# A recurrent, mixture-of-experts and attention network: expert rows scattered to their token's place, x kept in token rows, wide one-hots, feed-forward on chunk pairs

## The chip, the cores and the metric

The kernel runs on one core of a Trainium2 chip. The metric is the device time of one execution in microseconds. In the profile PE is TensorE's matmul side, PEld its weight loads, DVE is VectorE, ACT is ScalarE, POOL is GpSimd and SP is SyncE, whose queue issues most DMAs.

## The reference

There are 8 sequences of 256 steps with width 512. Floats are kept in pairs of 16-bit parts (high and low) in the kernel, so most products are done twice or three times.

```python
# GRU over time; here the 16x128 state sequence is the (8, 256, 512) input x
h = gru_scan(cond, x)                     # L0_cond, 256 steps, 8 sequences
scores = h @ w_gate_router.T             # 8 experts
topk_scores, topk_idx = top_k(scores, 2); p = softmax(topk_scores)
y = sum over the 2 experts of p * (silu(h @ gate_e.T) * (h @ up_e.T)) @ down_e.T   # F = 192
x = x + y                                                                          # called x1 below
xn = rms_norm(x) * g * (1 + scale) + shift      # scale, shift from cond @ W_emb, per sequence
q, k, v = xn @ W_qkv; q, k = rms_norm(q), rms_norm(k)   # 16 heads of 32
o = softmax(q k^T / sqrt(32)) v;  o = o + o @ W_out
hidden = sigmoid(o @ Q(w1).T) * (o @ Q(w2).T)   # Q: weights to -1, 0, 1; 1408 wide
x = x + hidden @ Q(w3).T
```

## The kernel before

**Layout.** The hidden states `hx` are kept with the features on the partitions and (time, feature block, sequence) in the free dimension. There are `NG = 16` groups of 128 tokens, in time order: a group holds 16 steps of all 8 sequences.

**Stages.** The recurrence runs to about 870 us. Then the states are split into 16-bit parts, scored by the router and written as token rows to DRAM (`xrows`), while weights arrive in pieces through `load_piece` and are split (to about 922 us). `slots` works out, for each token and each of its two experts, its place in a list sorted by expert, in which each expert's part is filled up to whole tiles of 128; there are `TILES = 40` tiles. To turn places into a list of rows, VectorE makes 32 one-hots of the place within the tile (`hot_low`, L1025), GpSimd 32 one-hots of the tile times the token's number (`hot_tile`, L1130), and `rows_of_tiles` (L758) multiplies them into `rowu`.

**Expert loop** (952 to 1117 us). For each tile GpSimd issues an indirect gather of 128 rows of `xrows` (L1138), TensorE transposes them (`turn_x`), multiplies by gate and up weights (`gate_up`, L778), transposes the hidden values and multiplies by the down weights (`down`). ScalarE evacuates (`take_y`, L896) and SP writes the tile to `yrows` in sorted order.

**Mix stage** (to 1178 us). For each of 16 groups GpSimd gathers the two expert rows of each token (L1147, slot by slot), ScalarE scales the first by its probability (L902), VectorE adds the second scaled (`mix_parts`, L1070), TensorE transposes back to features (`turn_back`, L811), VectorE adds x, which SP loads transposed (`residual`, L1076), ScalarE squares (L908), TensorE sums over partitions with a matrix of ones (`sum_x`), ScalarE takes the root (L914) and VectorE a reciprocal of 128 columns (`invert_x`, L1081).

**Attention** (to 1655 us). One batch is one sequence. `norm_x(b)` multiplies the states by the reciprocal root (VectorE, L1554), applies scale and shift per feature block (ScalarE, L1449, four operations), copies to 16 bits (L1453) and subtracts for the low part (L1556). It stands ahead of the stage for b = 0, at the end of the stage's start for b = 1, and at the end of batch b - 2 for the others, ahead of the eviction of the output projection (L1525, L1650). `project` (L1301) reads the result.

**Feed-forward** (to the end). Blocks of 128 hidden rows (`HM = 11`) of the ternary weights are quantised: GpSimd makes the negatives (L1188, three per block), VectorE finishes them (L1196). The first two blocks are done during attention. Tokens go in 4 chunks of 512. For each chunk, TensorE does for each block 16 matmuls into banks `mt % 2` (L1758); ScalarE takes the sigmoid (L1791), VectorE the product (L1816), ScalarE the high part (L1798) and VectorE the low part (L1820). Then 4 x 22 matmuls (L1774) give the result with features on partitions, VectorE adds x1 (L1828) and SP writes it out. Every engine keeps the order in which its instructions are written; semaphores tie the engines.

## Time and profile before

| | us |
|---|---|
| median of 3 runs | 1911.33 (1908.6 to 1915.46) |
| profiled execution | 1910.28 |
| its span | 1908.5 |

```profile
PE 1644.0 (86%) x31563; PEld 1199.2 (63%) x31563; DVE 1189.3 (62%) x4147; ACT 921.8 (48%) x3237; POOL 574.9 (30%) x1811
```

The line gives each engine's busy time, its share of the span and its instructions. The share is a mean over stages with different limits.

### The profile page before, as it was taken

Reading aid. Unit: us, or ns where it says so; the run is one execution under the profiler, and the core shown is the slowest. Engines: PE = TensorE matmul, PEld = TensorE weight load, DVE = VectorE, ACT = ScalarE, POOL = GpSimd, SP = SyncE. Lnnn points to the kernel's source line nnn. Section 1 sums busy time; section 2 is a strip of 40 time slices with the busy share of each in tenths; the row PEclk is TensorE's granted clock in tenths of the full one; section 3 lists DMA queues with packets and bytes.
Section 4 is the critical chain, followed back from the end, with each engine's and each line's share of the span. In section 5 each row is a group of like instructions: output and inputs, shape, how many; then the busy total and the mean of one; then the engine's idle time right before and its main releaser. Section 6 shows DMA issues by size and latency. Waiting matters only on the chain. (4 is left out here: it accounts for less than half of the span.)

```text
span 1908.5 us, 76620 instructions
## 1 busy us (share of the span) xinstructions
PE 1644.0 (86%) x31563; PEld 1199.2 (63%) x31563; DVE 1189.3 (62%) x4147; ACT 921.8 (48%) x3237; POOL 574.9 (30%) x1811
## 2 busy tenths in 40 slices
PE   6999999999999989994399965687888887689998
PEld 2788888888888889984256643354545555434443
DVE  4677777767777777777445436566666666573223
ACT  4544454445544444446245434367766666422111
POOL 0233333323333333334522234133322333660000
PEclk9898889988899955555599978789988988799999
DMA  7001000110000000005444356000000000220000
GB/s 273 26 4 50 5 26 5 60 44 5 4 5 5 18 35 5 4 5 169 137 149 143 130 164 193 1 1 0 0 0 0 0 0 1 65 77 13 22 22 22
DMA packets 39057, 90.19 MB, mean 47 GB/s; under 512 B 5088, under 2 KB 13408, under 8 KB 38624
## 3 DMA queue, kind: packets, MB, share of 16 engines
q1 hardware_dynamic: 32992, 66.96, 10.1%
q0 software_dynamic: 5760, 18.88, 3.4%
q8 instruction: 226, 3.70, 0.8%
q14 instruction: 79, 0.65, 0.1%
HBM read 66.88 MB, written 18.87 MB: 45 GB/s over the span
## 5 line engine op out<-in xcount | busy, mean ns | idle before, releaser
L321 PE MATMUL bank<-arena 128*128 128x8 f16 x12288 | 503.7, 171 | 32.4 <-DVE arena L500 27.2
L324 PE MATMUL bank<-arena 128*128 128x16 f16 x12288 | 498.1, 183 | 3.0 <-issue 2.7
L321 PEld LDWEIGHTS bank<-arena 128*128 128x128 f16 x12288 | 422.4, 99 | 85.0 <-ACT bank L409 57.3
L324 PEld LDWEIGHTS bank<-arena 128*128 128x128 f16 x12288 | 415.9, 99 | 3.7 <-issue 3.3
L573 POOL TENSOR_TENSOR arena<-arena 128x16 f32<-128x16 f32 x512 | 116.8, 228 | 597.8 <-DVE arena L504 583.2
L379 ACT ACTIVATE arena<-arena 128x16 f32<-128x16 f32 x512 | 114.2, 223 | 353.8 <-DVE arena L483 353.8
L483 DVE TENSOR_REDUCE arena<-bank 128x16 f32<-128x48 f32 x512 | 99.4, 194 | 147.3 <-PE bank L324 147.3
L1758 PE MATMUL bank<-arena 128*128 (+1 forms) x704 | 154.4, 379 | 15.5 <-DVE arena L1816 13.6
L1301 PE MATMUL bank<-arena 128*128 128x512 f16 x576 | 146.0, 409 | 17.5 <-DVE arena L1556 13.3
L494 DVE TENSOR_TENSOR_SCAN arena<-arena,bank 128x64 f32<-128x64 f32 x512 | 146.9, 287 | 20.4 <-ACT arena L379 6.0
L500 DVE TENSOR_TENSOR_SCAN arena<-arena 128x48 f16<-128x48 f32 x512 | 134.1, 262 | 6.0 <-ACT arena L389 0.6
L294 PE MATMUL bank<-arena 128*128 128x512 f16 x432 | 133.6, 423 | 0.0
L1758 PEld LDWEIGHTS bank<-arena 128*128 128x128 f16 x704 | 68.0, 98 | 101.2 <-DVE arena L1196 12.6
L389 ACT ACTIVATE arena<-arena 128x16 f32<-128x16 f32 x512 | 119.2, 233 | 24.7 <-DVE arena L494 4.7
L385 ACT ACTIVATE arena<-arena 128x16 f32<-128x16 f32 x512 | 110.3, 215 | 35.1 <-DVE arena L488 3.1
L488 DVE TENSOR_REDUCE arena<-bank 128x16 f32<-128x48 f32 x512 | 105.9, 207 | 26.3 <-PE bank L324 1.9
L1695 POOL TENSOR_TENSOR arena<-arena 128x512 f16<-128x512 f32 x64 | 79.3, 1247 | 130.6 <-ACT arena L1494 130.6
L504 DVE TENSOR_TENSOR_SCAN arena<-arena 128x48 f32<-128x48 f32 x512 | 117.1, 229 | 0.4
L1301 PEld LDWEIGHTS bank<-arena 128*128 128x128 f16 x576 | 59.5, 104 | 89.7 <-issue 24.5
L1791 ACT ACTIVATE arena<-bank 128x512 f32<-128x512 f32 x44 | 26.3, 597 | 176.1 <-PE bank L1758 176.1
L574 POOL COPY arena<-arena 128x16 f32<-128x16 f32 x512 | 110.9, 217 | 0.0
L509 DVE TENSOR_TENSOR arena<-arena 128x16 f16<-128x16 f32 x512 | 95.7, 187 | 17.7
(186 smaller groups left out, 2756.9 us busy)
## 6 DMA issues: line engine op xcount, KB each, us to landing
yrows<-arena SPq DMA_DIRECT2D x40, 256.0 KB
arena<-in_wgu SPq DMA_DIRECT2D x8, 768.0 KB, 5.9
arena<-in_xT SPq DMA_DIRECT2D x4, 1024.0 KB, 5.3
xrows<-arena SPq DMA_DIRECT2D x16, 256.0 KB, 4.8
arena<-in_xT SPq DMA_DIRECT2D x16, 256.0 KB
out_y<-arena SPq DMA_DIRECT2D x16, 256.0 KB, 2.0
arena<-in_wih SPq DMA_DIRECT2D x4, 768.0 KB, 8.6
arena<-in_whh SPq DMA_DIRECT2D x4, 768.0 KB, 5.2
```

The lines of the kernel that those rows point to most:

```text
L294: mm = nc.tensor.matmul(bank[7][:, :], wihs[:, wp, k, mt, :], xs[:, xp, k, :], start=(i % 12 == 0), stop=(i % 12 == 11))
L321: mm = nc.tensor.matmul(dst[:, j * B:(j + 1) * B, 1], w, h[:, 0], start=home not in opened, stop=False, skip_group_check=True)
L324: mm = nc.tensor.matmul(dst[:, j * B:(j + 1) * B, 1:3], w, h.rearrange("p a c -> p c a"), start=home not in opened, stop=False, skip_group ...
L379: A.activation(fn[:, HALF[g], 3], rzp[:, 0, HALF[g]], ACT.Sigmoid, scale=1 / SWX).then_inc(r_act[g], 1)
L389: A.activation(inh[:, HALF[g], 0], sn[:, HALF[g], 3], ACT.Tanh, scale=1 / SWX).then_inc(n_act[g], 1)
L494: V.tensor_tensor_scan(flat(sn[:, HALF[g]]), flat(fn[:, HALF[g]]), flat(gate_sums(t, 2, g)), 0.0, ALU.mult, ALU.add).then_inc(n_pre[g], 1)
L500: V.tensor_tensor_scan(flat(mv[:, t % 2, 0, HALF[g]]), flat(fh[:, HALF[g]]), flat(inh[:, HALF[g]]), 0.0, ALU.mult, ALU.add).then_inc(h_hi[ ...
L504: V.tensor_tensor_scan(flat(sh[:, HALF[g]]), flat(fh[:, HALF[g]]), flat(inh[:, HALF[g]]), 0.0, ALU.mult, ALU.add).then_inc(h_f32[g], 1)
L573: G.tensor_tensor(inh[:, HALF[g], 1], zeros[:, :], sh[:, HALF[g], 2], ALU.subtract)
L574: G.tensor_copy(inh[:, HALF[g], 2], sh[:, HALF[g], 2])
L1301: mm = nc.tensor.matmul(bank[5 + i % 2][:, :], xn[:, x_, k, half * P:(half + 1) * P], wqs[:, w_, k, col:col + D], start=(n == 0), stop=(n ...
L1758: mm = nc.tensor.matmul(bank[2 * a + mt % 2][:, :], w12[:, mt, a, k, :], o2p[:, part, k, bass.ts(c, CH)], start=(n == 0), stop=(n == 2 * K ...
```

## The change

**Scatter.** The list of rows now carries more: for each place the row of its token, whether it is the token's first or second expert (`pair`), and its probability in two parts. From these `goals` works out the row of `yrows` to which each place goes, `2 * token + (0 or 1)` in an order that puts tokens sequence by sequence; places that no token fills go to spare rows. `take_y` scales by the probability, and GpSimd scatters the tile with an indirect DMA. The two rows of one token thus lie side by side, and SP loads them for 128 tokens with one plain DMA.

**List of rows.** VectorE makes all one-hots in wide operations; GpSimd makes only two wide products for the probabilities (`hot_rest`), ahead of its gathers. `rest_of_tiles` stands on TensorE behind the first `gate_up`.

**Token rows.** x is loaded into SBUF as token rows (`xres`, over the states) during the expert loop. The two expert rows are added on GpSimd, the residual is added in token rows, and the sum of squares is along the free dimension (ScalarE, with an accumulated output). After the root and the reciprocal, ScalarE scales the rows, TensorE transposes them, and VectorE applies scale and shift on the way out of PSUM into `xnf`, for all sequences at once. `norm_x` is then only the split into two parts.

**Feed-forward.** Chunks go in pairs: for each block of weights the matmuls of two chunks. The down product takes the hidden values as weights and gives token rows. Loops over chunks are written out.

The core of the diff (constants, semaphores, memory layout and host arithmetic left out; `hdp` grows to two chunks):

```diff
-                for i in range(TILES):
-                    sp.wait_ge(y_evac, i + 1)
-                    sp.dma_start(yrows[i * P:(i + 1) * P, :], yo[:, i % 3, :]).then_inc(y_out[i % 3], 16)
+                sp.wait_ge(hc_lo, NG)
+                for g in range(NG):
+                    sp.dma_start(xres[:, g, :], xtok[g * P:(g + 1) * P, :]).then_inc(xres_in, 16)
...
+                    sp.dma_start(yb[:, g % 4], yrows[2 * g * P:2 * (g + 1) * P, :].rearrange("(p a) d -> p a d", a=2))\
+                        .then_inc(yb_in[g % 4], 16)
...
+                def rest_of_tiles():
+                    pe.wait_ge(slot_step, SLOT_STEPS["pair hot"])
+                    pe.wait_ge(part_hot, 2)
+                    for i in range(2 * NG):
+                        a, g = divmod(i, NG)
+                        mm = nc.tensor.matmul(bank[7][:, 0:3 * TILES], hot_low[:, a, g, :],
+                                              hot_rest[:, a, g].rearrange("p c t -> p (c t)"),
...
-                    A.activation(yo[:, i % 3, :], bank[6 + i % 2][:, :], ACT.Copy, scale=1 / SWX).then_inc(y_evac, 1)
+                    A.activation(yo[:, i % 3, :], bank[6 + i % 2][:, :], ACT.Copy, scale=share[:, i:i + 1]).then_inc(y_evac, 1)
+                def sum_squares(g):
+                    A.activation(square[:, :], xres[:, g, :], ACT.Square, accum_out=ssq[:, g:g + 1]).then_inc(sq_done, 1)
+                def root(g):
+                    A.activation(rms[:, g:g + 1], ssq[:, g:g + 1], ACT.Sqrt, scale=1 / D,
+                def unit_rows(g):
+                    A.activation(unit_x[:, g % 2, :], xres[:, g, :], ACT.Copy, scale=rinv[:, g:g + 1])\
...
-                    for i in range(2 * NG):
-                        a, g = divmod(i, NG)
-                        V.tensor_scalar(hot_low[:, a, g, :], iota, lowf[:, a, g:g + 1], None,
+                    V.tensor_tensor(hot_tile.rearrange("p a g t -> p (a g) t"),
...
+                    V.tensor_tensor(hot_row[:, :, :, :], hot_tile[:, :, :, :],
...
+                    for i in range(4):
+                        a, g = divmod(8 * i, NG)
+                        V.tensor_tensor(hot_low[:, a, g:g + 8, :], iota.unsqueeze(1).broadcast_to((P, 8, P)),
...
+                def residual(g):
+                    dve.wait_ge(ysum_done, g + 1)
+                    V.tensor_tensor(xres[:, g, :], xres[:, g, :], ysum[:, g % 2, :], ALU.add).then_inc(x1_done, 1)
+                def invert(g):
+                    V.reciprocal(rinv[:, g:g + 1], rms[:, g:g + 1]).then_inc(rinv_done, 1)
+                def adaptive(g):
+                    for k in range(KT):
+                        op = V.tensor_scalar(xnf[:, b, k, half * P:(half + 1) * P], bank[4 + g % 2][:, k * P:(k + 1) * P],
+                                             ada[:, 0, k, b:b + 1], ada[:, 1, k, b:b + 1], ALU.mult, ALU.add)
...
-                    G.tensor_scalar(hot_tile[:, a, g, :], iota[:, 0:TILES], tilef[:, a, g:g + 1], token[:, g:g + 1],
+                pool.wait_ge(slot_step, SLOT_STEPS["shares"])
+                for part in range(2):
+                    G.tensor_tensor(hot_rest[:, :, :, 1 + part, :], hot_tile[:, :, :, :],
+                                    prs[:, part].unsqueeze(3).broadcast_to((P, 2, NG, TILES)), ALU.mult)\
...
+                def scatter(i):
+                    pool.wait_ge(y_evac, i + 1)
+                    G.indirect_dma_start(out=yrows, out_offset=bass.IndirectOffsetOnAxis(ap=goal[:, i:i + 1], axis=0),
+                                         in_=yo[:, i % 3, :], in_offset=None).then_inc(y_out[i % 3], 16)
+                def sum_rows(g):
+                    pool.wait_ge(yb_in[g % 4], 16 * (g // 4 + 1))
+                    if g >= 2:
+                        pool.wait_ge(x1_done, g - 1)
+                    G.tensor_tensor(ysum[:, g % 2, :], yb[:, g % 4, 0, :], yb[:, g % 4, 1, :], ALU.add)\
+                for i in range(TILES + 6):
+                    if i < TILES:
+                        gather(i)
+                    if i >= 6:
+                        scatter(i - 6)
...
                 def norm_x(b):
-                    act.wait_ge(xnt_done, b + 1)
-                    for k in range(KT):
-                        A.activation(xnf[:, k, :], xnf[:, k, :], ACT.Identity, scale=ada[:, 0, k, bass.ds(b, 1)],
-                                     bias=ada[:, 1, k, bass.ds(b, 1)]).then_inc(xnf_done, 1)
-                    A.activation(xn[:, 0], xnf[:, :, :], ACT.Copy).then_inc(xn_hi, 1)
+                    A.activation(xn[:, 0].rearrange("p k s -> p (k s)"), xnf_of(b), ACT.Copy).then_inc(xn_hi, 1)
...
-                    V.tensor_tensor(xnf[:, :, :], x1, r, ALU.mult).then_inc(xnt_done, 1)
...
+                def up(pair, mt, cc):
+                    u, c = 2 * (pair * HM + mt) + cc, 2 * pair + cc
+                    if pair == 0 and cc == 0:
+                        pe.wait_ge(q_done, 3 * mt + 3)
+                    if u >= 2:
+                        pe.wait_ge(hdf_done, u - 1)
...
+                def down(pair, cc):
+                    for j in range(KT):
+                        v = (2 * pair + cc) * KT + j
+                        if v >= 2:
+                            pe.wait_ge(y_done, v - 1)
...
+                                mm = nc.tensor.matmul(bank[4 + j % 2][:, :], hdp[:, cc, part, mt, j * P:(j + 1) * P],
+                                                      w3q[:, mt, :], start=(n == 0), stop=(n == 2 * HM - 1))
...
+                for pair in range(2):
+                    for mt in range(HM):
+                        for cc in range(2):
+                            up(pair, mt, cc)
+                    for cc in range(2):
+                        down(pair, cc)
```

## Rows read from the trace of the kernel before

**Rows 1.** View by stretches: us, engines' busy us (instructions), granted TensorE clock, DMA share, GB/s
```profile
952.00:1117.00 165.00, 162.17 (x1192) 97.78 (x1191) 73.22 (x170) 78.59 (x166) 34.95 (x37) 0.99 0.41 134
1117.00:1178.00 61.00, 32.93 (x192) 25.93 (x192) 35.72 (x51) 25.76 (x49) 30.66 (x33) 0.83 0.73 211
```

**Rows 2.** Feed-forward stage: groups by line, whole run; then timeline and chain (start, us)
```profile
L1758 PE MATMUL bank<-arena 128*128 (+1 forms) x704 | 154.4, 379 | 15.5 <-DVE arena L1816 13.6 <-PEq L1266 1.8
L1774 PE MATMUL bank<-arena 128*128 128x512 f16 x352 | 77.3, 379 | 5.0 <-DVE arena L1828 5.0
...
1655.44 3.61 PE L1758 MATMUL bank<-arena 128*128 128x512 f16 x16 [1.83 <-PEq L1266]
...
1709.06 1.02 DVE arena L1828
1728.66 0.70 DVE arena L1816
1729.41 34.71 PE bank L1758 x160
1904.83 1.01 DVE arena L1828
```

**Rows 3.** Groups by line of 1655 to 1705 us: busy us, mean ns | idle before
```profile
L1188 POOL TENSOR_SCALAR arena<-arena,thr 128x512 f16<-128x512 f32 x27 | 43.4, 1625 | 12.8 <-POOLq L1266 12.4 <-DMA arena<-in_w3T 0.4
L1196 DVE SCALAR_TENSOR_TENSOR arena<-arena,thr 128x512 f16<-128x512 f32 x27 | 27.2, 1029 | 6.9 <-POOL arena L1188 6.9
L1820 DVE TENSOR_TENSOR arena<-arena 128x512 f16<-128x512 f32 x9 | 8.4, 938 | 0.0
```

**Rows 4.** Timeline where the list of rows is made: start us, us, engine, line
```profile
928.22 17.71 POOL L1130 TENSOR_SCALAR arena<-cst,arena 128x40 f16<-128x40 f32 x32 [12.22 <-DVE arena L1018]
928.37 6.37 DVE L1025 TENSOR_SCALAR arena<-cst,arena 128x128 f16<-128x128 f32 x32
...
946.79 1.17 POOL L1138 DMA_INDIRECT arena<-xrows,arena  x1 [0.87 <-DVE arena L1035]
```

**Rows 5.** Prices by width: VectorE groups by line, and GpSimd's L1126 (ns min/median/max)
```profile
L1010 DVE TENSOR_TENSOR arena<-arena 128x128 f32<-128x128 f32 x2 | 0.5, 288 | 0.0
L1028 DVE TENSOR_TENSOR arena<-cst,arena 128x320 f32<-128x320 f32 x1 | 0.5, 474 | 0.0
...
L1126 POOL TENSOR_TENSOR arena<-arena x16: 1147/1186/2204, 871.2 to 914.1; 128x512 f16<-128x512 f32 x16
```

**Rows 6.** View of the line that issues the gathers: ns min/median/max, time to landing
```profile
L1138 POOL DMA_INDIRECT arena<-xrows,arena x40: 941/944/1169, 946.8 to 1095.4; - x40
...
DMA to landing us min/median/max: 3.2/3.4/4.2
```

**Rows 7.** Timeline behind the experts: first gather, first use, and the last group's ring
```profile
1118.66 0.95 POOL L1147 DMA_INDIRECT arena<-yrows,arena  x1 [22.34 <-DMA yrows<-arena]
1123.46 0.72 ACT L902 ACTIVATE arena<-arena 128x512 f32<-128x512 f32 x1 [7.15 <-DMA arena<-yrows,arena]
...
1173.62 0.63 DVE L1076 TENSOR_TENSOR arena<-bank,arena 128x512 f32<-128x512 f32 x1
1174.28 0.63 ACT L908 ACTIVATE arena<-arena 128x512 f32<-128x512 f32 x1 [0.52 <-DVE arena L1076]
1176.16 0.37 ACT L914 ACTIVATE arena<-bank,epsb 128x128 f32<-128x128 f32 x1 [0.99 <-DVE arena L1081]
```

**Rows 8.** Timeline of the attention stage: first norm, second norm, end of a batch
```profile
1177.92 2.06 DVE L1554 TENSOR_TENSOR arena<-arena 128x1024 f32<-128x1024 f32 x1
1180.02 2.07 ACT L1449 ACTIVATE arena<-arena,ada 128x256 f32<-128x256 f32 x4 [3.49 <-DVE arena L1554]
1184.50 15.73 PE L1301 MATMUL bank<-arena 128*128 128x512 f16 x60 [8.38 <-DVE arena L1556]
...
1234.94 4.06 PE L1301 MATMUL bank<-arena 128*128 128x512 f16 x12 [4.96 <-DVE arena L1556]
...
1289.43 0.60 ACT L1525 ACTIVATE arena<-bank 128x512 f32 x1 [1.09 <-PE bank L1393]
```

More of the change, by code:

```diff
@@ L1785, in _, with gate, high @@
                 A = nc.scalar
[L1787 to L1802 removed]
+                def gate(u):
+                    act.wait_ge(up_mm, u + 1)
+                    A.activation(sgd[:, u % 2, :], bank[u % 2][:, :], ACT.Sigmoid, scale=1 / SX).then_inc(sgd_done, 1)
+                def high(u):
+                    pair, (mt, cc) = u // (2 * HM), divmod(u % (2 * HM), 2)
+                    act.wait_ge(hdf_done, u + 1)
+                    if pair == 1 and mt == 0:
+                        act.wait_ge(y_mm, (cc + 1) * KT)
+                    A.activation(hdp[:, cc, 0, mt, :], hdf[:, u % 2, :], ACT.Copy).then_inc(hdp_hi, 1)
+                for pair in range(2):
+                    for i in range(2 * HM):
+                        gate(2 * HM * pair + i)
+                        if i > 0:
+                            high(2 * HM * pair + i - 1)
+                    high(2 * HM * pair + 2 * HM - 1)
             @block.vector
@@ L1832, in _, with hidden @@
-                chunk(0, True)
-                with dve.Fori(1, NCH) as c:
-                    chunk(c, False)
-NAMES = ["xT", "condT", "wih", "whh", "bias", "wr", "wgu", "wdn", "wemb", "avec", "gqk", "wqkv", "wout",
+                def hidden(u):
+                    if u >= 2:
+                        dve.wait_ge(hdp_lo, u - 1)
+                    dve.wait_ge(sgd_done, u + 1)
+                    V.scalar_tensor_tensor(hdf[:, u % 2, :], bank[2 + u % 2][:, :], 1 / SX, sgd[:, u % 2, :], ALU.mult,
+                                           ALU.mult).then_inc(hdf_done, 1)
@@ new lines, in low, with result @@
+                def low(u):
+                    mt, cc = divmod(u % (2 * HM), 2)
+                    dve.wait_ge(hdp_hi, u + 1)
+                    V.tensor_tensor(hdp[:, cc, 1, mt, :], hdf[:, u % 2, :], hdp[:, cc, 0, mt, :],
+                                    ALU.subtract).then_inc(hdp_lo, 1)
+                def result(c, j):
+                    v = c * KT + j
+                    dve.wait_ge(y_mm, v + 1)
+                    if v >= 2:
+                        dve.wait_ge(y_out[j % 2], (c * 2 + j // 2) * 16)
+                    V.tensor_tensor(yo[:, j % 2, :], bank[4 + j % 2][:, :], xres[:, v, :], ALU.add).then_inc(y_done, 1)
@@ new lines, in _ @@
+                for pair in range(2):
+                    for i in range(2 * HM):
+                        mt, cc = divmod(i, 2)
+                        u = 2 * HM * pair + i
+                        if pair == 0 and mt + 2 < HM:
+                            quantise(dve, mt + 2, (0, 1) if cc == 0 else (2,))
+                        hidden(u)
+                        if i > 0:
+                            low(u - 1)
+                    low(2 * HM * pair + 2 * HM - 1)
+                    for c in (2 * pair, 2 * pair + 1):
+                        for j in range(KT):
+                            result(c, j)
```

368 lines of the change are left out of this document (173 added, 195 removed).

## Prediction

> **What bounds the kernel now.** I read the view by stretches first, cut where the stages end, then the chain that ended last, then the instruction timeline at the seams. The recurrence up to 870 us is not touched and neither is the splitting of weights and states up to 922 us. The expert loop is full of TensorE work: 162 of 165 us at a granted clock of 0.99 [rows 1]. The stage behind it is not: 61 us for sixteen row groups, with TensorE, VectorE and ScalarE each busy about half of it [rows 1]; work goes round in a ring there. In the last stage the chain is TensorE, broken by short waits [rows 2]. So each stage has a limit of its own, and each edit must be priced in its stage. The engines meet at the end of a stage, so a gain in one shifts all that follows.
>
> **Feed-forward on chunk pairs.** TensorE runs from 1655.44 us until the last add starts at 1904.83, some 249.3 us. It has 1056 matmuls of 512 columns in both kernels (704 up, 352 down); 160 in a row take 34.71 us, 0.217 each, so 229.2 us without waits. The idle time ahead of the two lines is 15.5 + 5.0 us [rows 2], which fits the difference of 20. Where it is: in the first chunk TensorE waits for the quantised weights, which GpSimd makes at 3 x 1.63 = 4.9 us per block [rows 3] against 3.47 us of matmuls; at the head of each later chunk the second block waits for the first one's sigmoid and product (the product is 0.70 us, [rows 2]); and the second result block waits for the first one's add (1.02 us, [rows 2]). With pairs a block of weights serves 32 matmuls, 6.94 us, so 4.9 us of GpSimd hide. Every wait on a bank then goes two units back, with 3.47 or 4.77 us of other matmuls between, so the head and the add hide too. What is late next is VectorE in the first pair: per block three quantisings (1.03 each), two low parts (0.94 each, [rows 3]) and two products (0.70, [rows 2]), 6.4 of 6.94 us. It fits, with little over; if it didn't, TensorE would pay at most the old first chunk's loss, some 10 us. The last add reads a contiguous residual instead of a strided one: 0.7, as the product, for 1.01 us [rows 2]. Sum: -20 - 0.3 = -20.3 us, bounds -10 and -21.
>
> **Attention.** norm_x loses a strided multiply on VectorE (2.06 us) and four scalings on ScalarE (2.07 us, after a wait) [rows 8]; a copy and a subtraction stay. At the stage's start nothing covers them: 2.06 + 2.07 = 4.1 us off the 6.6 between 1177.92 and 1184.50. For the second batch TensorE again sat idle until the norm was done (4.96 us ahead of 1234.94, [rows 8]) and ScalarE had the same work ahead of the first exponential: 4.2 us plus a wait, I take 4.7. In the other six batches it stood beside the output projection: ScalarE, done with the norm, still waited 1.09 us for TensorE [rows 8], so I take nothing there (bounds 0 and -5 for six). Sum: -8.8.
>
> **Behind the experts.** Removed per group: two gathers on GpSimd's queue, a load of x, a scaled copy, a mix, a strided sum, a strided square, four ones-matmuls and a 128-wide reciprocal. Added: one 512 KB load from SP, a sum on GpSimd, a contiguous residual add, a square with an accumulated sum, a root and a reciprocal of one column, a scaled copy, four transposes, and four 128-column operations of VectorE that apply scale and shift. The ring of one group is residual (0.63), square (0.63, with 0.1 to 0.2 for the accumulated sum, which no row shows), root (0.37 for 128 columns, I take 0.25 for one), reciprocal (0.2, as VectorE's narrow operations: 6.37 us for 32, [rows 4]) and some 0.07 us for each of four handovers: 2.1 us [rows 7]. The apply (4 x 0.2 by the same row) stands in VectorE's gap while ScalarE works; the GpSimd sum of group g+2 is released by residual g and runs in the same gap. Sixteen groups are 33.6 us. The start comes later: the final tile must be scattered (0.94 us of issue, 3.2 to 4.2 to land by the gathers, [rows 6]) and a 512 KB load must land. Before, 4.8 us went from the first gather to its use [rows 7]; I set the first sum at 1125 us, 1.1 for it, 33.6, and 3 for the last copy, transposes and apply: 1162.7 against 1177.9, -15. Bounds: if the transfers set it, 8.4 MB at the 211 GB/s of this stage [rows 1] are 40 us and the gain is 11; if GpSimd and VectorE hinder each other on every group (a GpSimd subtraction of 512 columns took 1.15 to 2.20 us, [rows 5]), 0.7 us more each leaves 4; at best -18.
>
> **The list of rows.** Before, 32 GpSimd one-hots take 17.71 us from 928.22 while VectorE needs 6.37 for its 32; the first gather is issued at 946.79 [rows 4]. Now VectorE does all in wide operations. Its price is some 1.0 ns per column plus 0.16 (128 columns 0.288, 320 columns 0.474, [rows 5]): two of 1280 columns are 2.9, four of 1024 are 4.7, the two small splits 0.4, so 936.4; the last eight matmuls and the cast end near 938. But GpSimd has two products of 1280 columns queued ahead of its gathers: 2.25 to 4.3 ns per column [rows 5] are 5.8 to 11 us from 932, 938 to 943. I take 940: -7, bounds -4 and -9.
>
> **Added in the expert loop.** 32 matmuls of 120 columns stand once on the full TensorE, 0.05 us each by columns and 0.1 at half clock: 1.6 to 3.3 us, and eight small VectorE steps behind them hold the first hidden tile back by about 0.5. I take +3.3. The stores move from SP to GpSimd: a gather costs it 0.94 us [rows 6] and some 0.3 to the next, so gather and scatter are 2.5 of 4.1 us per tile and hide. The scatter of tile j waits for an evacuation that TensorE reaches before it frees the next gather, so no gather is held. A stored tile has three buffers, about 12 us, against 6 for issue and landing. SP loads x, 4 MB, beside it; the loop's DMA share is 0.41 [rows 1]; I take +1, bounds 0 and 4.
>
> The Trainium skill speaks against moving stores to GpSimd ("SBUF — State Buffer", section "SBUF: two separate sides"): a VectorE operation in a two-port mode locks GpSimd out and a DMA issue that takes about 620 ns takes about 3100. By that figure gather plus scatter would be some 4.6 us, estimated from the page, above the 4.1 of a tile. The gathers' 941 to 1169 ns do not show it.
>
> **Sum.** -20.3 - 8.8 - 15 - 7 + 3.3 + 1 = -46.8 us. The profiled run took 1910.28 (span 1908.5), so 1863.5; the median of the three runs is 1 us above it: 1864.5.
>
> **Rivals.** (a) Units queue in the first pair, VectorE having 0.5 us left of 6.94 per block: +9, 1873. For it: [rows 3] shows VectorE slowed beside GpSimd. Against: the two-unit distance. 0.10. (b) The stage behind the experts is held by transfers or by GpSimd against VectorE: +4 to +11, 1868 to 1876. For it: a DMA share of 0.73 before. Against: 8.4 MB for the 12.6 of before, in larger pieces. 0.12. (c) GpSimd paces the expert loop. A scatter is free up to 2.5 us of issue; at 3.1 each tile takes 0.6 more, +24, 1888. The slowest gather was 1.17 us, and only a scatter unlike any gather would do it. This is also the outcome of the page named above. 0.05. (d) Slower than before: the same place, if the issue exceeds 3.7 us, from where 40 tiles cost more than 47 us; at 4.2 it gives 1864.5 + 67 = 1931. 0.03. (e) The edit doesn't do what it says: GpSimd's two products hold the gathers as long as the old one-hots did, +7, 1872; no row has so slow a product. 0.03. (f) More than I count: norms in all eight batches and a faster ring, 1846 to 1851. 0.07. The forecast itself, 1853 to 1873: 0.60.
>
> **Range and chances.** 1850 to 1882 takes in (a), (b), (e) and most of (f). A measurement of this kernel tells about 0.3% (6 us) from no change. Faster by more: 0.95; within: 0.02; slower by more: 0.03.
>
> **What the changed profile would show.** TensorE idle ahead of the up and down matmuls under 3 us in all, and the last stage near 230 us: pairs right. First gather near 940 and the first gate matmul 4 us later: list right; GpSimd's products ending after 943: (e). A scatter's mean near 0.95 us and tiles 4.1 apart: else (c) or (d). Groups 2.1 us apart behind the experts: my ring; 2.5 and waits for the load: (b). The first projection some 2.5 us into its stage, the batches as long as before. The prediction falls if the expert loop lengthens by over 10 us, or if the ring has a member I missed.

## The result and the profile after

| | before | after |
|---|---|---|
| median | 1910.84 us (1908.6 to 1915.46, 4 runs) | 1866.78 us (1865.92 to 1867.83, 4 runs) |
| profiled execution, its span | 1910.28, 1908.5 us | 1867.83, 1866.0 us |

The ratio is 0.9762, with an interval of 0.9749 to 0.9775: 44 us less, inside the range and 2.3 us above the forecast. The spans differ by 42.5 us.

The view by stretches of the kernel after, cut where its stages end (columns as in [rows 1]): the expert loop, the stage behind it, attention, and feed-forward.

```profile
948.30:1113.90 165.60, 163.27 (x1216) 98.75 (x1216) 73.63 (x177) 82.20 (x166) 75.95 (x76) 0.99 0.45 157
1113.90:1167.50 53.60, 17.57 (x64) 11.57 (x64) 34.12 (x96) 27.39 (x66) 21.20 (x17) 0.54 0.48 166
1167.50:1634.70 467.20, 377.23 (x3592) 234.01 (x3593) 280.53 (x504) 287.62 (x477) 155.01 (x121) 0.85 0.02 6
1634.70:1863.50 228.80, 228.08 (x1056) 103.23 (x1056) 91.25 (x131) 50.53 (x89) 45.29 (x27) 1.00 0.13 45
```

Set beside the same places of before, taken in order from 922 us on, this makes the table that the rest of the text explains. The boundaries are start times, so that the stretches add up (for instance, the first gate matmul starts at 948.26 for 952.91, and the last result add, which closes feed-forward, at 1862.82 for 1904.83). after_again is the same kernel, profiled a second time.

| stretch | predicted | measured, after | measured, after_again |
|---|---|---|---|
| up to 922 us (untouched) | 0 | +0.6 | +3.0 |
| list of rows, to the first gate matmul | -7 | -5.3 | -5.2 |
| expert loop, to the last `take_y` | +3.3 and +1 | +2.2 | +2.1 |
| behind the experts, to the start of attention | -15 | -7.9 | -8.6 |
| attention | -8.8 | -10.4 | -13.1 |
| feed-forward | -20.3 | -21.3 | -21.3 |
| last add and store | 0 | -0.4 | -0.4 |
| sum | -46.8 | -42.5 | -43.5 |

Each sum meets its difference of spans. Between the two traces of one kernel the untouched part differs by 2.4 us and attention by 2.7, in opposite directions, so in these two rows a difference of under 3 us does not tell of the change; the other rows agree to 0.7 us. Of the kernel before there is one trace only.

The last stage is the largest term. The chain that ended last in the kernel after, over that stage (start us, us, what):

```profile
1634.70 76.13 PE bank L1834 x352
1710.84 37.99 PE bank L1850 x176
1748.83 75.97 PE bank L1834 x352
1824.80 38.00 PE bank L1850 x176
...
1862.82 0.69 DVE arena L1907
```

It is TensorE without a break from 1634.70 to 1862.80 us, 228.1 us for 1056 matmuls, where [rows 2] had 249.3 with 20.5 us of waits. The last add is 0.69 us for 1.01.

### The profile page after: what moved, and what is told of

It is laid out like the page before. It is cut to its first block and busy times, and to the rows that moved or that the text cites. A ratio compares the mean times of both kernels' runs of the same rounds, so it can differ in the third digit from the quotient of the medians.

```text
span 1866.0 us, 76127 instructions
## 1 busy us (share of the span) xinstructions
PE 1624.7 (87%) x31467; PEld 1188.2 (64%) x31467; DVE 1169.3 (63%) x4173; ACT 909.2 (49%) x3221; POOL 598.5 (32%) x1805
## 5 line engine op out<-in xcount | busy, mean ns | idle before, releaser
L501 DVE TENSOR_TENSOR_SCAN arena<-arena,bank 128x64 f32<-128x64 f32 x512 | 146.8, 287 | 20.5 <-ACT arena L386 6.0
L1834 PE MATMUL bank<-arena 128*128 128x512 f16 x704 | 152.3, 379 | 1.7 <-PEq L1355 1.7
L1390 PE MATMUL bank<-arena 128*128 128x512 f16 x576 | 145.9, 409 | 4.5 <-DVE arena L1634 4.5
L301 PE MATMUL bank<-arena 128*128 128x512 f16 x432 | 132.9, 421 | 0.0
L1834 PEld LDWEIGHTS bank<-arena 128*128 128x128 f16 x704 | 68.8, 98 | 84.7 <-issue 1.9
L581 POOL COPY arena<-arena 128x16 f32<-128x16 f32 x512 | 110.8, 216 | 0.0
L582 POOL COPY arena<-arena 128x16 f32<-128x16 f32 x512 | 102.9, 201 | 0.0
```

Of the source, the lines that this page charges most:

```text
L301: mm = nc.tensor.matmul(bank[7][:, :], wihs[:, wp, k, mt, :], xs[:, xp, k, :], start=(i % 12 == 0), stop=(i % 12 == 11))
L501: V.tensor_tensor_scan(flat(sn[:, HALF[g]]), flat(fn[:, HALF[g]]), flat(gate_sums(t, 2, g)), 0.0, ALU.mult, ALU.add).then_inc(n_pre[g], 1)
L581: G.tensor_copy(inh[:, HALF[g], 2], sh[:, HALF[g], 2])
L1390: mm = nc.tensor.matmul(bank[5 + i % 2][:, :], xn[:, x_, k, half * P:(half + 1) * P], wqs[:, w_, k, col:col + D], start=(n == 0), stop=(n ...
L1834: mm = nc.tensor.matmul(bank[2 * a + u % 2][:, :], w12[:, mt, a, k, :], o2p[:, 2 * c:2 * c + 2, part, k, :], start=(n == 0), stop=(n == 2 ...
```

## The list of rows: what held VectorE's one-hots

The stage gained 1.7 us less than predicted, and not for the reason that I gave. The timeline of the kernel after where the list is made:

```profile
932.25 8.89 DVE L1070 TENSOR_TENSOR arena<-cst,arena 128x1024 f16<-128x1024 f32 x4
932.41 6.51 POOL L1203 TENSOR_TENSOR arena<-arena 128x1280 f16<-128x1280 f16 x2 [16.50 <-DVE arena L1067]
...
942.17 1.17 POOL L1210 DMA_INDIRECT arena<-hrows,arena  x1 [3.25 <-DVE arena L1079]
```

GpSimd's products ended at 938.92 and it then sat idle for 3.25 us, so the gathers did not wait for GpSimd, as my sum had it. They waited for VectorE: its four one-hots of 1024 columns took 8.89 us and not 4.7. The matmuls that each of the first three releases show where: these ended just ahead of 933.61, 936.79 and 940.06, and the last at 941.14, so the second and third took 3.2 us each and the first and fourth 1.2. The records of the two products and of the second and third one-hot, one by one:

```profile
932.41 3.24 POOL L1203 TENSOR_TENSOR arena<-arena 128x1280 f16<-128x1280 f16 x1 [16.50 <-DVE arena L1067]
933.38 3.35 DVE L1070 TENSOR_TENSOR arena<-cst,arena 128x1024 f16<-128x1024 f32 x1
935.61 3.31 POOL L1203 TENSOR_TENSOR arena<-arena 128x1280 f16<-128x1280 f16 x1
936.65 3.35 DVE L1070 TENSOR_TENSOR arena<-cst,arena 128x1024 f16<-128x1024 f32 x1
```

The products end at 935.65 and 938.92. The second one-hot ends 1.08 us behind the first product and the third one-hot 1.08 us behind the second product, which is about the length of a one-hot that nothing disturbs. Each product in turn ends 2.2 us behind the one-hot before it. So the two engines took turns, and each long record holds the other's instruction and then its own. Two experiments take the products away from these one-hots, one to a later place on GpSimd, one to VectorE itself.

**list_pool_late.** The two products stand behind the third gather:

```diff
-                pool.wait_ge(slot_step, SLOT_STEPS["shares"])
-                for part in range(2):
-                    G.tensor_tensor(hot_rest[:, :, :, 1 + part, :], hot_tile[:, :, :, :],
...
                 for i in range(TILES + 6):
+                    if i == 3:
+                        pool.wait_ge(slot_step, SLOT_STEPS["shares"])
+                        for part in range(2):
+                            G.tensor_tensor(hot_rest[:, :, :, 1 + part, :], hot_tile[:, :, :, :],
...
                     if i < TILES:
                         gather(i)
```

> The changed kernel with one thing moved: GpSimd's two wide products for the probabilities stand behind its first three gathers instead of ahead of all of them. Theory A (VectorE's wide one-hots wait for GpSimd): in the changed kernel the four one-hots of 1024 columns took 8.89 us instead of 4.7, and their results came 3.2 us apart while a product of 3.27 us ran; without the products beside them they take 4.6 to 4.9 us, the first gather is issued near 938.1 instead of 942.17, and the run is some 3 to 4 us shorter than the changed kernel's 1866.8. Rival B (the wide one-hots are slow by themselves, for their repeated operands): they stay at 8.9 us and the gather stays at 942.

Measured: 1861.87 us, ratio 0.9721 (0.9705 to 0.9738). Its timeline in the same place:

```profile
931.28 4.63 DVE L1070 TENSOR_TENSOR arena<-cst,arena 128x1024 f16<-128x1024 f32 x4
...
936.95 1.17 POOL L1205 DMA_INDIRECT arena<-hrows,arena  x1 [21.15 <-DVE arena L1079]
...
940.65 4.61 POOL L1228 TENSOR_TENSOR arena<-arena 128x1280 f16<-128x1280 f16 x2
```

The one-hots take 4.63 us, 1.16 each: my price by width (4.7) was right for VectorE alone. The products, with no one-hots beside them, take 4.61 us for 6.51. From the start of the first wide one-hot to the first gather are 8.92 us (928.03 to 936.95), where the kernel after has 13.17 (929.00 to 942.17): 4.2 us less. Added up, the one-hots and the products by themselves are 4.63 + 4.61 = 9.24 us; beside each other, from 932.25 to 941.14 us, they took 8.89, so next to nothing overlapped.

**list_dve.** The same two products are VectorE's, behind its other work on the list:

```diff
                 owners()
+                dve.wait_ge(slot_step, SLOT_STEPS["shares"])
+                for part in range(2):
+                    V.tensor_tensor(hot_rest[:, :, :, 1 + part, :], hot_tile[:, :, :, :],
...
```

> The changed kernel with the two wide products made by VectorE, behind the cast of the list, while the first gathers are on their way; GpSimd has no work ahead of its gathers. Theory A: one-hots 4.6 to 4.9 us, first gather near 938.1, two products of about 1.5 us each hidden behind the landing of the first gather; about 4 us shorter than the changed kernel, as the variant with late products or 0 to 1 us better. Rival B: as the changed kernel.

Measured: 1862.31 us, ratio 0.9726 (0.971 to 0.9742). The timeline:

```profile
937.89 1.17 POOL L1210 DMA_INDIRECT arena<-hrows,arena  x1 [20.16 <-DVE arena L1079]
...
938.64 2.89 DVE L1174 TENSOR_TENSOR arena<-arena 128x1280 f16<-128x1280 f16 x2
939.36 1.59 POOL L1210 DMA_INDIRECT arena<-hrows,arena  x1 [0.30 <-issue]
```

The first gather comes as early (8.9 us after the first wide one-hot), and the products are 2.89 us on VectorE. The second and third gather are issued in 1.59 and 1.09 us, where the rows of the kernel after have 0.95: VectorE's products slow GpSimd too, by 0.8 us here. The two kernels can't be told apart by their times.

What follows: the first gather was held by VectorE, which was held by GpSimd. The Trainium skill ("SBUF — State Buffer", section "SBUF: two separate sides") says that VectorE and GpSimd share a pair of SBUF ports as a lock for a whole instruction, whichever starts first, and that a VectorE operation with two SBUF inputs takes part in it against a GpSimd operation that reads SBUF. By that rule, the trace agrees: one-hots and products took turns, whole instructions at a time, and without the products all four one-hots take 1.16 us.

## The expert loop: is the scatter hidden?

Predicted: gather and scatter together are 2.5 of 4.1 us per tile. The view of the two lines that issue them, in the kernel after (ns min/median/max, first and last start):

```profile
L1210 POOL DMA_INDIRECT arena<-hrows,arena x40: 942/968/1171, 942.2 to 1093.0; - x40
L1216 POOL DMA_INDIRECT yrows<-arena x40: 969/987/1583, 962.6 to 1114.2; - x40
```

The 40 tiles' `take_y` run from 961.2 to 1113.3 us, 152.1 us, against 963.7 to 1115.7, 152.0, before. The loop's cost is at its head only. `rest_of_tiles` took

```profile
951.34 1.84 PE L798 MATMUL bank<-arena 128*128 128x120 f16 x32
```

in the lower half of my 1.6 to 3.3. That SP's loads of x cost 1 us does not show.

**plain_store** puts the stores back on SP, in the order of the list, and leaves the gathers alone:

```diff
-                    G.indirect_dma_start(out=yrows, out_offset=bass.IndirectOffsetOnAxis(ap=goal[:, i:i + 1], axis=0),
-                                         in_=yo[:, i % 3, :], in_offset=None).then_inc(y_out[i % 3], 16)
+                    pass
...
+                for i in range(TILES):
+                    sp.wait_ge(y_evac, i + 1)
+                    sp.dma_start(yrows[i * P:(i + 1) * P, :], yo[:, i % 3, :]).then_inc(y_out[i % 3], 16)
```

> Leaves out the scatter: the 24 tiles of expert rows are stored by SyncE in the order of the list, so the rows behind the experts are added to other tokens' x, and the output is not the reference's. Everything else keeps its work. Theory (the scatter is hidden, and only its last issue counts): the tile period of the expert loop stays at 4.02 us, gathers keep their 0.97 us, and the stage behind the experts starts 0.5 to 1.5 us earlier, 1865 to 1867 us. Rival (GpSimd's second duty costs in the loop, through the gathers or through what VectorE loses beside it): the loop of 24 tiles shortens by over 3 us, 1864 us or less.

(There are 40 tiles; the 24 in this text is a slip.) Measured: 1867.33 us, ratio 0.9759 (0.9744 to 0.9774), beside 1867.71 us and 0.9769 (0.9755 to 0.9782) for the changed kernel in the same session:

> The changed kernel again, in the session of the three that follow, so that they have a neighbour. Expected 1866 to 1871 us, and a ratio of 0.976 to the kernel before.

The `take_y` of plain_store run over 153.1 us, those of after_again over 152.2, so the loop is not shorter without the scatter. (The edit also moves SP's loads of x and of the last weight pieces in between the stores; the 0.9 us by which the loop is longer lies within what other kernels with an unchanged loop show, 151.9 to 153.0 us.) The first GpSimd sum comes 6.2 us after the last `take_y` in plain_store and 7.0 us in after_again: 0.8 us, the price of the last issue. The rival falls: GpSimd's second duty costs nothing in the loop. The slowest scatter took 1.58 us, far from the 2.5 at which it would have begun to count; the slow issue that was weighed as a rival did not come. The figure of about 3100 ns that the Trainium skill gives for a DMA issued from GpSimd beside a VectorE copy ("SBUF — State Buffer", section "SBUF: two separate sides"; the page gives it for the DMA, and the prediction took it for the issue) is shown by no run here; the slowest issue was the 1.59 us in list_dve.

## Behind the experts: the member of the ring that I missed

Here the prediction was off by 7 us. The timeline of the kernel after over one pair of groups (DVE L1141 is the residual, ACT L937 square and accumulator, L941 root, L948 scaled copy, PE L854 the transposes, DVE L1151 scale and shift, L1145 the reciprocal):

```profile
1153.13 0.67 DVE L1141 TENSOR_TENSOR arena<-arena 128x512 f32<-128x512 f32 x1
...
1153.84 0.63 ACT L937 ACTIVATE arena<-arena 128x512 f32<-128x512 f32 x1 [0.30 <-DVE arena L1141]
...
1154.38 0.19 ACT L937 ACTIVATION_READ_ACCUMULATOR arena<-arena 128x1 f32 x1
1154.59 0.29 ACT L941 ACTIVATE arena<-arena,epsb 128x1 f32<-128x1 f32 x1
1154.75 1.36 DVE L1151 TENSOR_SCALAR arena<-bank,ada 128x128 f32<-128x128 f32 x4 [0.94 <-PE bank L854]
...
1156.10 0.67 DVE L1141 TENSOR_TENSOR arena<-arena 128x512 f32<-128x512 f32 x1
...
1158.06 0.67 DVE L1141 TENSOR_TENSOR arena<-arena 128x512 f32<-128x512 f32 x1
```

Residuals stand 2.97 us apart (1153.13 to 1156.10), then 1.96 (to 1158.06), and so on in turn; 16 of them from 1121.49 to 1161.03 make 2.64 on the mean, where I had 2.1. The terms themselves were priced well: residual 0.67, square 0.63, accumulator 0.19 (no row of before had shown it), root 0.29, reciprocal 0.15. In every second group VectorE sits idle for 0.94 us ahead of L1151, waiting for the transposes of the group two back, and the reciprocal of the present group, which ScalarE needs, and the next residual are queued behind it.

The first gap is longer than all others, 4.27 us, and had no term in my sum:

```profile
1121.49 1.79 DVE L1141 TENSOR_TENSOR arena<-arena 128x512 f32<-128x512 f32 x1 [11.35 <-POOL arena L1223]
...
1124.05 1.28 ACT L941 ACT_TABLE_LOAD   x1
```

The first residual stood beside GpSimd's second sum (to 1122.73 us) and ended 0.55 us behind it, taking 1.79 us instead of 0.67, and ScalarE spent 1.28 us on a load ahead of its first root.

The candidates for the longer gap in every second group are the order of VectorE's instructions and the two banks of the transposes. ring_deep changes both, the other two one each.

**ring_deep, ring_order, ring_banks.** The first half of the edit is the order, in ring_order and ring_deep:

```diff
-                for g in range(NG + 2):
+                for g in range(NG + 3):
                     if g < NG:
                         residual(g)
-                    if g > 1:
-                        adaptive(g - 2)
+                    if g > 2:
+                        adaptive(g - 3)
```

The second is the banks, in ring_banks and ring_deep (`adaptive` reads the same banks):

```diff
-                    if g >= 2:
-                        pe.wait_ge(xnf_done, g - 1)
+                    if g >= 4:
+                        pe.wait_ge(xnf_done, g - 3)
...
-                        mm = nc.tensor.transpose(bank[4 + g % 2][:, k * P:(k + 1) * P],
+                        mm = nc.tensor.transpose(bank[4 + g % 4][:, k * P:(k + 1) * P],
```

> The changed kernel with VectorE's scale-and-shift step taken three groups behind instead of two, and four banks for the transposes instead of two. Theory C (the ring of the stage behind the experts is set by VectorE waiting 0.94 us for the transposes in every other group): groups come 2.2 to 2.4 us apart instead of 2.64 on average, and the stage is 4 to 6 us shorter. Rival D (the loads or GpSimd's sums set the pace): the groups stay 2.6 apart, the waiting moves to the sum or the load, and nothing is gained.

> The changed kernel with one half of ring_deep: VectorE applies scale and shift to group g-3 instead of g-2 behind the residual of group g; the transposes keep their two banks. Theory (VectorE's order is the cause: in the changed kernel the operation on group g-2 waits 0.94 us for its transposes, with the reciprocal of group g queued behind it): groups 1.96 us apart as in ring_deep, and 40 to 42 us from the first GpSimd sum to the stage's end, where the changed kernel has 47 to 49; 1859 to 1862 us. Rival (the two banks are the cause): the order alone gains under 2 us, since transposes then wait for the operation on the group two back.

> The changed kernel with the other half of ring_deep: four banks for the transposes, VectorE's order as it was. Theory (VectorE's order is the cause; in the changed kernel's rows the transposes wait for ScalarE only, never for a bank): no change, groups alternate between 1.96 and 2.97 us, 1866 to 1869 us. Rival (the banks are the cause): groups 1.96 us apart, 1859 to 1862 us.

| kernel | us | ratio | first GpSimd sum to first projection |
|---|---|---|---|
| after | 1866.78 | 0.9762 | 49.7 us |
| after_again | 1867.71 | 0.9769 | 49.0 us |
| ring_deep | 1861.77 | 0.9715 (0.9699 to 0.9731) | 41.9 us |
| ring_order | 1861.30 | 0.9714 (0.9698 to 0.973) | 41.9 us |
| ring_banks | 1866.94 | 0.9743 (0.9727 to 0.9759) | 49.0 us |

The timeline of ring_order:

```profile
1149.10 0.69 DVE L1141 TENSOR_TENSOR arena<-arena 128x512 f32<-128x512 f32 x1
...
1149.71 1.35 DVE L1151 TENSOR_SCALAR arena<-bank,ada 128x128 f32<-128x128 f32 x4
...
1151.06 0.69 DVE L1141 TENSOR_TENSOR arena<-arena 128x512 f32<-128x512 f32 x1
```

and of ring_banks:

```profile
1148.08 0.67 DVE L1141 TENSOR_TENSOR arena<-arena 128x512 f32<-128x512 f32 x1
...
1150.04 0.67 DVE L1141 TENSOR_TENSOR arena<-arena 128x512 f32<-128x512 f32 x1
...
1151.66 1.36 DVE L1151 TENSOR_SCALAR arena<-bank,ada 128x128 f32<-128x128 f32 x4 [0.95 <-PE bank L854]
```

With the order alone the wait ahead of L1151 is gone and the groups behind the third stand 1.96 us apart; with the banks alone nothing moves. By the traces the order gives the whole 7 us, more than ring_deep was expected to give, and it is settled: VectorE's order of instructions is the cause. The two kernels were run beside each other, and ring_order is 5.6 us faster by the medians; no run of one comes near a run of the other (1862.12 us at most, 1865.27 at least). (The ratio of ring_banks lies below that of after_again, with intervals that overlap; its stage does not differ.) With the first gap of 4.27 us and the others at 1.89 to 2.03, the mean in ring_order is 2.11, what I had priced at 2.1. The DMA share of the stage in ring_deep is 0.58 at 192 GB/s, so neither transfers nor GpSimd set its pace.

## Attention: was the removed norm work hidden in the loop?

I took 4.1 us at the first norm, 4.7 at the second and nothing in the other six batches. The total was 10.4. Starts of the operation that opens a batch (ACT L1477 before, L1560 after), as lengths in us; the five middle periods are added up:

| | start of stage to first projection | to batch 0 | period 0 | periods 1 to 5 | period 6 | batch 7 to feed-forward |
|---|---|---|---|---|---|---|
| before | 6.6 | 41.7 | 54.15 | 273.65 | 53.78 | 47.6 |
| after | 2.4 | 42.1 | 51.39 | 272.25 | 52.46 | 46.6 |
| after_again | 2.4 | 40.8 | 49.24 | 273.65 | 52.37 | 46.0 |
| norm_in_loop | 2.4 | 41.5 | 49.50 | 273.75 | 53.80 | 47.5 |

The first norm is as predicted: 4.2 us, and the first projection 2.4 us into the stage. The second is 4.9 in after_again, but 2.76 in after. The timeline of after shows where a part of it went:

```profile
1215.68 4.98 PE L1390 MATMUL bank<-arena 128*128 128x512 f16 x12
```

Twelve matmuls of 512 columns took 4.98 us, where [rows 8] has 4.06 behind its 4.96 us of idle time and after_again has 4.15. Period 0 as a whole, in after and then in after_again (columns as in [rows 1]):

```profile
1212.03:1263.42 51.39, 42.43 (x401) 25.54 (x401) 32.15 (x59) 35.48 (x58) 17.56 (x14) 0.80 0.01 1
1212.45:1261.69 49.24, 38.92 (x401) 22.95 (x401) 31.99 (x59) 35.50 (x58) 17.59 (x14) 0.88 0.01 2
```

The same 401 matmuls kept TensorE busy for 42.43 us at a granted clock of 0.80 and for 38.92 at 0.88. So the idle time is gone in both, but in after TensorE was longer at the lower of its two levels, and 2.2 us of the gain went there. No experiment here shows why two executions of one kernel differ in this. The five middle periods are the same in before and in after_again (273.65 us); the 1.4 us less in after stands in no other trace.

**norm_in_loop** puts the removed work back, on scratch, for the six batches whose norm stands beside the output projection, on ScalarE ahead of the high halves and on VectorE ahead of the low ones:

```diff
+                    if extra:
+                        act.wait_ge(probs, b)
+                        for k in range(KT):
+                            A.activation(scr[:, k, :], scr[:, k, :], ACT.Identity, scale=ada[:, 0, k, bass.ds(b, 1)],
+                                         bias=ada[:, 1, k, bass.ds(b, 1)])
...
+                    if extra:
+                        V.tensor_tensor(scr[:, :, :], x1, x1, ALU.mult).then_inc(probs, 1)
```

> Puts the work that the change took from each batch's norm back for batches 2 to 7: VectorE multiplies 2048 elements ahead of the low halves, and ScalarE scales four times 512 ahead of the high ones, on scratch, so nothing that the output depends on changes. Theory (in the loop the norm lies beside the output projection and was hidden before the change): no change, within 1 us, batch periods of 54.4 us as in the changed kernel. Rival (the batches gained from the removal): 0.5 us or more for each of six batches, 3 us or more in all, 1870 us or more.

(The operations put back have the sizes that the change removed, 1024 columns on VectorE and four times 256 on ScalarE; the 2048 and 512 in this text are slips.) Measured: 1871.36 us, ratio 0.9784 (0.9769 to 0.9799), 3.6 us above after_again. So "no change" was wrong, and the rival's "0.5 us for each batch" was wrong too. The last batch of the loop in norm_in_loop, from 1536.81 us (ACT L1614 and DVE L1738 evict the output projection, PE L1391 is the next batch's projection):

```profile
1541.14 2.07 ACT L1540 ACTIVATE arena<-arena,ada 128x256 f32<-128x256 f32 x4 [3.02 <-DVE arena L1641]
...
1546.21 2.76 PE L1391 MATMUL bank<-arena 128*128 128x512 f16 x12 [1.05 <-DVE arena L1738]
```

and the same place in after_again, from 1535.34 us:

```profile
1540.78 0.60 ACT L1608 ACTIVATE arena<-bank 128x512 f32 x1 [3.19 <-PE bank L1482]
...
1543.53 2.75 PE L1390 MATMUL bank<-arena 128*128 128x512 f16 x12
```

With the work in place the evictions come late and the next projection waits for them: it starts 9.40 us after the batch's opening (1546.21) instead of 8.19 us (1543.53). In a middle batch it is 9.41 against 8.62, and there the second projection follows 4.0 us later instead of 4.8, so it starts at the same place and the delay is gone; the five middle periods differ by 0.1 us in all. In the last batch of the loop the projections follow each other at 3.4 us in both kernels, there is no gap to absorb it, and period 6 is 1.43 us longer. The kernel before shows the same period, 53.78. So the norm was hidden in five batches and cost 1.4 us in one. The stretch behind batch 7 is 1.5 us longer as well (47.5 and 47.6 with the work, 46.0 without), although no extra work stands in it. Its first 5.3 us in norm_in_loop and in after_again, and the 24 matmuls of the output projection with which it opens, in norm_in_loop and in after_again:

```profile
1590.61:1595.91 5.30, 4.64 (x23) 3.30 (x23) 1.72 (x3) 1.31 (x4) 0.00 (x0) 0.50 0.01 2
1587.72:1593.02 5.30, 4.77 (x32) 3.77 (x33) 1.69 (x3) 1.90 (x4) 0.00 (x0) 0.69 0.01 2
...
1591.27 5.02 PE L1483 MATMUL bank<-arena 128*128 128x256 f16 x24 [0.70 <-DVE arena L1701]
...
1588.25 4.12 PE L1482 MATMUL bank<-arena 128*128 128x256 f16 x24 [0.56 <-DVE arena L1692]
```

With the work in place the granted clock is 0.50 over these 5.3 us (0.51 in before), without it 0.69, and 1.0 us of the difference arises here. Matmul by matmul the rest of the stretch runs at equal distances up to its last 6 us, where the granted clock is 0.86 for 0.93 and the other 0.5 us arises. So the 1.5 us lie where TensorE is longer at the lower level. That the later period 6 brings this about is likely, and no experiment shows it.

## Feed-forward: what the pairs give

**ffn_unpaired** keeps the new order of waits and the token rows, but takes the chunks one by one, as before the change:

```diff
-                for pair in range(2):
-                    for mt in range(HM):
-                        for cc in range(2):
-                            up(pair, mt, cc)
-                    for cc in range(2):
-                        down(pair, cc)
+                for c4 in range(NCH):
+                    for mt in range(HM):
+                        up(c4 // 2, mt, c4 % 2)
+                    down(c4 // 2, c4 % 2)
```

(and the same order on ScalarE and VectorE).

> The changed kernel with its feed-forward taken chunk by chunk again, while the waits on the banks, the token-row product and the written-out loops stay. Theory E (of the 21.3 us gained in the last stage some 10 come from pairs of chunks that hide the quantising, and 10 from waits that go two units back): 9 to 11 us slower than the changed kernel, all of it in the first chunk, where TensorE waits for the weights; no waits at the heads of the later chunks. Rival F (all is in the waits and the order of banks, the pairs bring nothing): the same time as the changed kernel. Rival G (all is in the pairs): 20 us slower, with waits of about 1.4 us at each chunk's head.

Measured: 1879.7 us, ratio 0.9815 (0.9798 to 0.9831) to the kernel before, and 12.9 us above the kernel after, which was run at another time. The chain that ended last in it (POOL L1272 makes the negatives):

```profile
1649.55 4.57 POOL arena L1272 x3
...
1678.57 3.61 PE bank L1834 x16
1682.18 18.99 PE bank L1850 x88
1701.17 37.99 PE bank L1834 x176
...
```

In the first chunk the chain is GpSimd, 4.83 us from block to block (4.57 of work and 0.26 to the next), as [rows 3] led me to expect; from 1678.57 us on it is TensorE without a break. The stage is 238.9 us long (1633.2 to 1872.13) against 228.1. So the pairs hide GpSimd in the first chunk and give 10.8 us; the other half of the gain, 249.3 - 238.9 = 10.4 us, comes without pairs. In the trace of before, TensorE waits 1.42 us for a product at the head of each of the three later chunks, and 1.10 to 1.31 us for an add in each of the four chunks, 9.3 us in all; in ffn_unpaired none of these waits is left. The code says why: before, the second block of a chunk waited for the first one's product, and the second result for the first one's add, since the banks were counted anew in each chunk; now units alternate between the banks across chunks and always wait for the unit two back.

The rival that units queue in the first pair falls by the groups of 1634 to 1716 us in the kernel after:

```profile
L1834 PE MATMUL bank<-arena 128*128 128x512 f16 x352 | 76.1, 379 | 1.7 <-PEq L1355 1.7
L1272 POOL TENSOR_SCALAR arena<-arena,thr 128x512 f16<-128x512 f32 x27 | 45.3, 1694 | 19.6 <-POOLq L1355 12.2 <-DVE arena L1280 7.2 <-DMA arena<-in_w3T 0.2
L1280 DVE SCALAR_TENSOR_TENSOR arena<-arena,thr 128x512 f16<-128x512 f32 x27 | 24.2, 918 | 2.4 <-POOL arena L1272 2.4
```

TensorE's idle time ahead of L1834 is 1.7 us, all ahead of the stage. VectorE's operations are no slower than I priced them: 918 ns for 1029, and 708 for 938 in the low parts (L1899).

## Two edits together

**both_pool** joins list_pool_late and ring_deep.

> Two edits of the first set together: GpSimd's two products go behind the third gather, and the transposes behind the experts rotate over four banks, with the residuals three groups ahead of the applications. Theory: the two gains lie in stages that follow each other and share nothing, so they add: first gather 4 us earlier than in the changed kernel, groups behind the experts 1.96 us apart instead of 2.64 on the mean, 7 to 8 us in that stage; together 9 to 12 us, 1855 to 1859 us, ratio 0.970 or lower by the changed kernel's own spread. Rival: one of the two is given back later, through TensorE's granted clock in the expert loop or in the first batches of attention, and the time stays where ring_deep alone stood, within 1 us.

Measured: 1856.52 us, ratio 0.9708 (0.9695 to 0.9721), 11.2 us below after_again, run beside it. By the traces the first 1024-column one-hot to the first gather is 5.7 us for 9.9 in after, and the first sum to the first projection is 41.9 us for 49.0 in after_again: 4.2 and 7.1, 11.4 us together. Attention from its first projection to feed-forward is 462.3 us for 462.0, so nothing was given back. It is faster than the kernel before by 2.9% and than the changed kernel by 0.6%.

The single edits' times are 5.8 and 5.9 us below after_again, but they were taken in another session, in which the kernel before ran 2.5 us slower; for them I rely on the stages.

## Why the prediction was right, step by step

- **Feed-forward** (-20.3, measured -21.3): right, with both halves in their place (9.4 us of waits in the first chunk of before, 9.3 behind it). The text gave the pairs the credit for the heads of later chunks and the adds; ffn_unpaired shows that this half is the order of banks.
- **Attention** (-8.8, measured -10.4, and -13.1 in after_again): first norm right (4.2 for 4.1). Second right in after_again (4.9 for 4.7), 2 us too much in after, through the clock. "I take nothing there" for the last six was wrong for the last of them: the wait of 1.09 us in [rows 8] was read in the first batch and held for five of the six. It was 1.4 us in period 6, and 1 to 1.6 us behind it, where TensorE is longer at the lower level.
- **Behind the experts** (-15, measured -7.9): the failed step. "The apply (4 x 0.2 by the same row) stands in VectorE's gap while ScalarE works". It took 1.36 us, not 0.8, and, what counts, it can't start when the gap begins: its transposes are late, and it holds the reciprocal behind it. By parts: pace 16 x (2.64 - 2.1) = +8.6; the first sum 7.0 us after the last `take_y` where I had 9.3 (1125 against 1115.7), -2.3; last sum to end of stage +1.0. That makes the 7.3 us by which the term, counted from the end of the loop, was too large. With the order alone changed, in ring_order, the stage is 15.7 us shorter than before, so the order accounts for the whole miss (the first gap, 2.2 us longer than a group was priced, is made up by the others, which are some 0.1 us shorter each). The work was sized from rows, but VectorE's queue was not written out in order.
- **List** (-7, measured -5.3): I named GpSimd's products as what holds the gathers, at 940 us. The first gather came at 942.2, held by VectorE. The sign given for rival (e), products ending after 943, did not come, since it named the wrong engine. The price of the widths was right (4.63 for 4.7 us alone).
- **Expert loop** (+4.3, measured +2.2): the matmuls 1.84 us; the 0.4 left I put to the small steps behind them, which no run tests; the loads nothing that shows.

The misses were +7.1 behind the experts and +1.7 on the list, against -2.1 in the loop, -1.6 in attention and -1.0 in feed-forward. The sum was closer than its terms, and that much of it was luck: a miss of 8.8 us in one direction met 4.7 in the other. Of the rivals, (b) had the right place and a size of 4 to 11 us but named transfers or contention; the cause was a third one in that place, and contention shows in the first groups only (1.79 us for a residual that takes 0.67).

Two workings of the prediction don't come out. Transfers of 40 us in place of the ring's 33.6 leave a gain of 8.8 us by the sum's own terms, not 11. And the range from 1850 us takes in only 1 us of (f), 1846 to 1851, not most of it. Neither touches the forecast.

## What to carry to other kernels

When two engines hand work back and forth, write out the in-order queue of each engine for two rounds, with the time at which each instruction's input is ready. A step of 1.4 us that fits a gap by its length still lengthens the ring if its input comes late and the next round's first step is queued behind it; the cure may be to take it one round later, at no cost in buffers. And when wide VectorE operations replace narrow ones, look at what GpSimd does beside them, since each may then be held for the length of the other's instruction: price such a pair as the sum of the two.

## What the runs showed of the hardware

- A VectorE product of a constant and a broadcast row, 1024 columns, took 1.16 us alone. Beside GpSimd's products of 1280 columns the two engines took turns by whole instructions: a held one-hot ended 1.08 us behind the product (record of 3.35 us), and a product took 3.27 us for 2.33 without. Four one-hots and two products, 9.24 us one by one, took 8.89 together.
- Two products of 1280 columns took VectorE 2.89 us and GpSimd 4.61: moving the two to VectorE cost 0.8 us of gather issues and nothing in the time.
- An indirect store is issued as fast as an indirect load: 987 ns at the median for 968, and 1583 for 1171 at worst.
- ScalarE's accumulated sum costs a separate read of 0.19 us behind the square of 0.63. Its first square root behind the squares had a table load of 1.28 us ahead of it.
- VectorE's scale and shift out of PSUM, 128 columns with two values per partition, takes 0.34 us each by four in a row (1.36).
